# Macaron block (FFN, attention, FFN): even back chunks placed six lines later, odd ones loaded a body ahead

## What is computed

```python
x = x + 0.5 * ffn(layernorm(x))
x = x + attn(layernorm(x))
x = x + 0.5 * ffn(layernorm(x))
```

```python
q, k, v = bitnet_linear(x, q_weight, q_scale), bitnet_linear(x, k_weight, k_scale), bitnet_linear(x, v_weight, v_scale)
scores = einsum('bhqd,bhkd->bhqk', q, repeat(k, 4)) / sqrt(16)
out = einsum('bhqk,bhkd->bhqd', softmax(scores), repeat(v, 4))
return bitnet_linear(out.reshape(b, s, 512), o_weight, o_scale)
```

## Time and profile before

| what | value |
|---|---|
| median of 3 executions | 1163.4 us (1157.81 to 1164.84) |
| the profiled execution, its own time | 1162.77 us |
| its span (first to last instruction) | 1161.0 us |
| mean granted TensorE clock | 0.959 of full |
| PE busy | 1061.4 us, 91% |
| DVE busy | 837.9 us, 72% |
| ACT busy | 727.0 us, 63% |
| POOL busy | 295.4 us, 25% |

### The profile page before, as it was taken

One profiled execution on the slowest core, in us unless ns is written; L12 is line 12 of the kernel. 1 busy time (PEld: TensorE's weight loads), 2 busy tenths in 40 slices (PEclk: granted clock), 3 DMA queues, 4 the chain that ended last, 5 costly groups with the idle time before them and its releaser, 6 DMA issues.

```text
span 1161.0 us, 16018 instructions
## 1 busy us (share of the span) xinstructions
PE 1061.4 (91%) x5776; PEld 466.8 (40%) x5776; DVE 837.9 (72%) x1107; ACT 727.0 (63%) x1361; POOL 295.4 (25%) x485
## 2 busy tenths in 40 slices
PE   5989887999999999999999999999999999999647
PEld 4778661344334422333334333433343334233236
DVE  5766679767777777876787778777877887871274
ACT  6556432757865786675676667666767675768311
POOL 5355546302420240410050023003200420041010
PEclk9989886999999999999999999999999999999869
DMA  7122331021211123111211121121113010301300
GB/s 254 46 81 88 100 103 49 27 73 36 60 49 35 33 59 105 31 32 48 87 31 31 61 75 31 31 87 48 31 31 110 30 40 17 115 10 33 108 0 37
DMA packets 70507, 68.31 MB, mean 59 GB/s; under 512 B 15132, under 2 KB 52508, under 8 KB 70428
## 3 DMA queue, kind: packets, MB, share of 16 engines
q1 hardware_dynamic: 70428, 67.29, 18.9%
HBM read 41.95 MB, written 24.63 MB: 57 GB/s over the span
## 4 chain that ended last, share of the span: by engine, by line
PE 72%; DVE 13%; ACT 5%; DMA 3%; issue 3%; POOL 3%; SPq 1%; DVEq 0%; ACTq 0%; POOLq 0%
PE ps_out L1516 19%; PE ps_score L1504 18%; PE ps_max L1485 16%; PE ps_fill L1441 5%; DVE neg_max L1312 5%; ACT probs L1018 2%; PE ps_fill L1470 2%; PE ps_fill L1423 2%; PE ps_fill L1445 1%; DVE neg_max L1110 1%; DVE zd L1184 1%; PE ps_out L1441 1%; PE ps_fill L1409 1%; PE ps_fill L1415 1%; DVE xn L1252 1%
## 5 line engine op out<-in xcount | busy, mean ns | idle before, releaser
L1018 ACT ACTIVATE probs<-ps_score 128x512 f32<-128x512 f32 x992 | 539.0, 597 | 262.0 <-PE ps_score L1504 260.9
L1312 DVE TENSOR_REDUCE neg_max<-ps_max 128x1 f32<-128x1024 f32 x480 | 570.9, 1219 | 179.7 <-PE ps_max L1485 177.7
L1504 PE MATMUL ps_score<-qst,kst 99*128 99x512 bf16 x992 | 308.9, 387 | 10.1 <-ACT probs L1018 8.5
L1485 PE MATMUL ps_max<-kst,qst 96*128 96x512 bf16 x1024 | 290.1, 389 | 16.8 <-DVE neg_max L1110 5.8
L1516 PE MATMUL ps_out<-probs,v_ring 128*32 128x512 f32 x2048 | 274.7, 608 | 7.3 <-ACT o_sb L1027 4.9
L1504 PEld LDWEIGHTS ps_score<-qst,kst 99*128 99x128 bf16 x992 | 76.0, 97 | 273.6 <-ACT probs L1018 232.4
L1485 PEld LDWEIGHTS ps_max<-kst,qst 96*128 96x128 bf16 x1024 | 91.4, 99 | 144.5 <-issue 19.5
L852 POOL CAST shift<-neg_max 128x16 bf16<-128x16 f32 x32 | 9.2, 286 | 435.0 <-DVE neg_max L1312 430.6
L1516 PEld LDWEIGHTS ps_out<-probs,v_ring 128*32 128x32 f32 x2048 | 40.9, 108 | 95.6 <-issue 87.2
L948 ACT ACTIVATE xn<-xc,ln_shift,rstd 128x512 f32<-128x512 f32 x48 | 38.6, 814 | 30.6 <-POOL ln_shift L748 19.6
L1441 PE MATMUL ps_fill<-wb_h,xt_h 128*128 128x512 f32 x84 | 47.1, 561 | 1.0 <-DVE xc L1299 0.8
(11 more groups left out here) (254 smaller groups left out, 1296.6 us busy)
## 6 DMA issues: line engine op xcount, KB each, us to landing
qst<-q_dram SPq DMA_DIRECT2D x192, 64.0 KB, 2.2
att_dram<-o_sb SPq DMA_DIRECT2D x31, 256.0 KB, 2.1
q_dram<-zm SPq DMA_DIRECT2D x24, 256.0 KB, 2.6
kst<-k_dram SPq DMA_DIRECT2D x192, 32.0 KB, 2.2
xc<-x SPq DMA_DIRECT2D x8, 512.0 KB, 4.0
x_dram<-xc SPq DMA_DIRECT2D x8, 512.0 KB, 2.9
xc<-x_dram SPq DMA_DIRECT2D x8, 512.0 KB, 5.6
out<-xc SPq DMA_DIRECT2D x8, 512.0 KB, 3.1
```

The source lines that it names most:

```text
L1018: act.activation(probs[:, kt % 2, j, :], score_bank(i, uu, j), ACT.Exp, scale=1.0 / HD ** 0.5).then_inc(probs_ready, 1)
L1312: dve.tensor_reduce(neg_max[:, uu % 2, t:t + 1], ps_max[max_slot(uu, pos)][:, :, :], AXY, ALU.max, negate=True).then_inc(max_read, 1)
L1485: last = pe.matmul(ps_max[slot][:, half, :], qst[0:SR, r, j, q * P:(q + 1) * P], kst[0:SR, r, half * 512:half * 512 + 512], start=True, st ...
L1504: pe.matmul(score_bank(i, uu, j), kst[0:SR + PARTS, uu, kt * P:(kt + 1) * P], qst[0:SR + PARTS, uu, j, :], start=True, stop=True).then_inc ...
```

## The change

The steps `N0a`, `N0al`, `N0b`, `N0bl` move from lines 15, 16, 16, 17 to 13, 15, 17, 19, so that DVE has one of them in each of four slots. All steps of even chunks move six lines (three slots) on, and those that pass the end of the body go to the first lines of the next body (line 63 is folded into 62). For odd chunks `NR` and `NL` move to lines 54 and 57 of the body before, and the attention output is loaded at slot 24 of the body before. An odd chunk's `load_x1` moves from slot 4 to slot 8. The calls of `body` on all engines change only in the plan that they get; one of six such places is shown.

```diff
-    8 * [""] + ["NR", "NL", "", "", "", "", "", "N0a", "N0al N0b", "N0bl", "", "Oa0", "Oa1", "C0", "Ob0", "Ob1", "", "G0 C1", "P0", "", "G1", "P1",
+    8 * [""] + ["NR", "NL", "", "", "", "N0a", "", "N0al", "", "N0b", "", "N0bl Oa0", "Oa1", "C0", "Ob0", "Ob1", "", "G0 C1", "P0", "", "G1", "P1",
...
+LINES = 2 * UB * KT
+EVEN_SHIFT = 6
+EARLY = {"NR": 54, "NL": 57}
...
-        def back_plan(chunk):
-            return {k: [(chunk, step) for step in line] for k, line in enumerate(BACK)}
+        def back_plan(i):
+
+            plan = {}
+            for n in range(max(i - 3, 0), min(i - 1, LOOP_BACKS - 1) + 1):
+                for k, line in enumerate(BACK):
+                    for step in line:
+                        at = LINES * (n + 2) + k + (EVEN_SHIFT if n % 2 == 0 else 0)
+                        if n % 2 == 1 and step in EARLY:
+                            at = LINES * (n + 1) + EARLY[step]
+                        if at // LINES == i:
+                            plan.setdefault(min(at % LINES, LINES - 2), []).append((Chunk("back", 0, n), step))
+            return plan
...
-                    if slot == 2 and load_next is not None:
+                    if slot == 2 and load_next is not None and load_next.n % 2 == 0:
                         if load_next.n > 0:
                             sp.wait_ge(filler_ready[0], Chunk("back", 0, load_next.n - 1).written("T1b"))
                         load_att(load_next)
-                    if slot == 4 and load_next is not None:
+                    if slot == 24 and load_next is not None and load_next.n % 2 == 0:
+                        if load_next.n > 0:
+                            sp.wait_ge(att_low_ready[0], 2 * load_next.n)
+                        load_att(Chunk("back", 0, load_next.n + 1))
+                    if load_next is not None and slot == (8 if load_next.n % 2 else 4):
                         load_x1(load_next, chunk_loaded[0])
...
             for i in range(2, 7):
                 ch = Chunk("back", 0, i - 2)
-                body(i, back_plan(ch), ch)
+                body(i, back_plan(i), ch)
```

More of the change, by code:

```diff
@@ L681, in _ @@
                 ch = Chunk("back", 0, i - 2)
-                body(i, back_plan(ch), ch)
+                body(i, back_plan(i), ch)
             ch = Chunk("back", 0, 5)
-            body(7, back_plan(ch), ch, last=True)
+            body(7, back_plan(7), ch, last=True)
             for ch in tail:
@@ L897, in _ @@
             for i in range(2, 7):
-                body(i, back_plan(Chunk("back", 0, i - 2)))
-            body(7, back_plan(Chunk("back", 0, 5)), last=True)
+                body(i, back_plan(i))
+            body(7, back_plan(7), last=True)
             for item in tail_steps():
@@ L1050, in _ @@
             for i in range(2, 7):
-                body(i, back_plan(Chunk("back", 0, i - 2)))
-            body(7, back_plan(Chunk("back", 0, 5)))
+                body(i, back_plan(i))
+            body(7, back_plan(7))
             copy_out(8, -1)
```

## The result

The change makes the kernel slower: 1176.6 us (median of 4; 1172.26 to 1179.31) against 1162.7 (median of 4), a ratio of 1.0115 with a 95% interval of 1.0087 to 1.0143. It is just past the 1% that was called no change, and the interval reaches to both sides of that 1%; no change had been given 0.72, and slower than that 0.21. The profiled execution took 1179.3 us.

What follows compares the result with a forecast made beforehand. PE, busy 91% of the span, was taken to bound the kernel. Odd chunks -3.4, even chunks +9.7 and the rest -1.3 sum to +5.0 us on 1162.77, 1167.8, said as 1168 us; range 1154 to 1180.

Steps and rivals of the forecast that it cites:

- the prize: Slots 7 to 10 of six bodies: 14.97 us in all above the 13.66 us each takes without waiting, 1.3% of the time.
- Part 1: The four spread steps: N0a's 1.05 us lag stays, slot 9's 0.76 falls to 0.2; 1.25 us excess per body, not 1.81.
- Part 2: Bodies 3, 5 and 7: inverse sums sent a body earlier, so body 3's transfer wait goes; gain 3.4 us.
- Part 3: Bodies 2, 4, 6: reload behind twelve q and k loads; DVE waits 3.4 us at N0a, plus 1.2 for clock; loss 9.7.
- third rival: SP, end of slot 8, even bodies: store slow behind q and k loads, 7.1 us wait, +19.8 us, 1183 us; chance 0.15.
- Part 4: The rest, moved inversion, layer norm, FFb and PE filler: a gain of 1.3 us, between a loss and a gain of 3.
- reload in time: Rival: N0a in slot 10 of even bodies finds its data, only 1.25 us left per body; -8.8, 1154 us; chance 0.15.
- collision of the shifted chunk: Rival: POOL's guard at slot 15 and FFa2 to FFa4 in line 62 cost some 2 us per even body; 1174 us; 0.12.
- slow store: Rival at SP's slot 8 end, even bodies: landing 4.6 us, reload 5.9, N0a waits 7.1; 1183 us; chance 0.15.
- All of the excess goes: Rival: the lag at N0a is hidden too; -14.97 us and a little more, 1147 us; chance 0.06.

Runs made afterwards that it cites:

- e1: The change with even chunks' inversion, store and reload of the inverse sums left at lines 8 and 9, ahead of slot 8's q and k loads; 1156.64 us.
- e6: e1 with ACT's casts N0a and N0b one line later, DVE and all else as in e1; 1147.58 us, ratio 0.9873.
- e3: The change plus 18 matmuls with unused results on PE at the end of slot 10 of bodies 2, 4 and 6; 1168.91 us.
- e5: The change with EVEN_SHIFT = 0, so even chunks stay at their own lines; 1168.25 us.
- e2: The change with SP issuing even bodies' store and reload of the inverse sums at the head of slot 8, before the q and k loads; 1161.54 us.
- e4: The kernel before with only the new places of the four steps, no shift and no early load; 1179.1 us.

## Why the prediction was right or wrong

**What bounds the kernel, and the prize.** Right. PE was busy for 91 or 92% of the span before, after and in e1, and the stretches of slots named there hold the whole difference: 14.97 us of excess before, and after it 3 x (15.11 - 13.66) = 4.35 in odd bodies and 9.62 + 9.67 + 8.23 = 27.5 in even ones, 16.9 more; the span grew by 16.5. e6 recovered nearly all of the prize (its stretches have 0.7 us of excess left), and came out 15 us below the kernel before.

**Part 1, one step in a slot.** The lag of 1.05 us at N0a stayed, as said. The excess was 1.45 us in odd bodies and 1.69 in even ones (e1), where 1.25 was forecast.

**Part 2, odd chunks.** Right in place and mechanism; the gain was 7.11 - 4.35 = 2.8 us against 3.4.

**Part 3, even chunks: the wait.** Right, term by term, in body 2: the store went out 4.8 us into slot 8 (forecast 4.8), the reload 1.74 after it (1.8), and it landed 5.6 later (5.0); DVE's turn was 8.2 us into slot 8 (8.2). The wait was 3.97, 3.91 and 4.10 us where 3.4 was taken, because the landing was taken 0.5 to 0.7 too short (it took 5.6, 5.5 and 5.7).

**Part 3: the clock. This is the term that was mis-sized.** The prediction had it in the right place, behind the wait, and charged it with a fixed price: "I charge a wait of DVE for a transfer at its length plus 1.2 us." That came from two rows, behind waits of 0.47 and 1.13 us. Measured against e1, the stretch of body 2 lost 22.96 - 15.03 = 7.93 us, of which 3.97 was the wait: 3.96 for the rest. In body 4 it was 4.07 and in body 6 2.44. That is 10.5 us where 3.6 were charged, and it accounts for 6.9 of the 11.5 us by which the span's growth exceeds the forecast's +5.0. PE's busy time tells the same: in these stretches it is 18.02, 18.13 and 16.50 us, against 13.96 in e1 for the same matmuls. So does the granted clock: 0.78 over 22.96 us means some 10 us at the lower of the two levels (0.22 x 22.96 x 2), against about 3.6 us in the stretch of body 2 before (0.10 x 17.90 x 2). e3 shows the cause: with PE busy through the wait, body 2 lost 4.11 us for a wait of 4.02.

The price was not too small because these waits are longer. Body 4 of e5 lost 4.1 us behind a wait of 1.30, and body 2 of e5 only 2.0 behind one of 3.58 (the table at the end has more). Such a price is not a constant, and two rows that agreed on 1.2 and 1.3 could not show that. The third rival, which charged 2.4, tied it to the length too.

The remaining 4.6 us of the 11.5 are the longer wait (1.8), the larger residue of part 1 (1.9) and what was missing of part 4 (0.9).

**Part 4.** A gain of 1.3 us was taken; about 0.4 is seen (16.9 in these stretches, 16.5 in the span). In that are 1.1 us lost to one more stretch of lower clock, in slot 17 of body 7 of this execution, and 0.2 by which body 2 began later. Without these two the rest of the kernel gained 1.7 us, and in e1, counted from the start of body 2, it gained 1.7 as well: the term was about right.

**The rivals.** The reload in time did not happen in the change, but its arithmetic was close: it gave 1154 us, and e1, where the reload is in time, took 1156.6. The collision of the shifted chunk is refuted by e1: all of the shift is in it but the inversion and the reload of the sums. The slow store did not occur (1.74 to 1.78 us); that its rival would decide above a wait of 5.3 us does not follow from the prediction's own sum, which reaches 11.6 us at 3.4 + (11.6 - 5.0) / 3 = 5.6. "All of the excess goes" gave 1147 and was held unlikely because "ACT's place relative to DVE's is unchanged"; e6 changed that place and took 1147.6.

**The chances.** By the profiled execution the time rose 16.5 us, by the medians 13.9. With the measured 10.5 us of clock in place of 3.6 the same sum gives 1168 + 6.9 = 1175. The range held, because its upper end was set by another path, a slow store, which did not occur; the forecast's own ends moved the wait and part 4 and kept the clock at 1.2 us, so no change got too much.

## What to carry to other kernels

A step that moves by lines in a table moves past other queues' work too: count what stands ahead of it on the queue that issues its transfers, here 12 loads of 0.46 us each. Put a store, a reload and whatever waits for them on one line of time (issue, landing, issue, landing, use) before moving any of them, and leave room: margins under a slot were what four bodies had. Charge a wait on TensorE's path with its length and a range on top, and not a fixed price: behind waits of 0.9 to 4.1 us these runs lost between 0.1 and 4.1 us more. And where two engines hand a tile over in the same slot, place the receiver behind the giver's real lag, after which the giver's load in a slot matters.

## What the runs showed of the hardware that was not expected

- What the lower clock costs behind a wait is not a function of the wait's length, nor of how long PE stood idle. The last column is the stretch of four slots, less the same slots without a wait (15.03 us for even bodies with the shift, 15.11 for the new order without it, 15.47 before), less the wait. What decides between these was not tried.

| kernel, body | DVE's wait, us | PE idle, us | granted clock | lost beyond the wait, us |
|---|---|---|---|---|
| e2, 4 | 0.90 | 1.87 | 1.00 | 0.1 |
| before, 2 | 1.13 | 2.18 | 0.90 | 1.3 |
| e5, 4 | 1.30 | 2.36 | 0.75 | 4.1 |
| e2, 6 | 1.41 | 2.38 | 1.00 | 0.1 |
| e2, 2 | 1.46 | 2.43 | 0.90 | 1.4 |
| e4, 7 | 1.71 | 2.77 | 0.75 | 3.9 |
| e5, 2 | 3.58 | 4.64 | 0.84 | 2.0 |
| the change, 2 | 3.97 | 4.94 | 0.78 | 4.0 |
| the change, 6 | 4.10 | 5.07 | 0.84 | 2.4 |

- The granted clock also differs between executions of one kernel, and the time with it: the two executions of the change with a mean granted clock of 0.949 took 1179.3 us, the two with 0.955 and 0.956 took 1173.89 and 1172.26.
- Extra work can shorten a kernel: 54 unused matmuls, about 12.5 us of PE's time (18.14 - 13.96 = 4.2 in body 2), took 7.7 us off the change's median (1176.6 to 1168.91; 6 us by the ratios), since PE kept its clock through two of the three waits and most of the third.
- A reload of 4 x 128 KB from DRAM landed 5.5 to 5.7 us after its first issue with one store and the shift rows issued behind it (the change), and 6.7 us with the loads of q and k right behind it (body 2 of e2).
